# Cross-attention's orders of work on five engines replaced by others, the mask's load set between the context's halves

## What is computed

```python
qp = (q @ Wq.T + bq).reshape(b, t_q, h, d // h).transpose(0, 2, 1, 3)
kp = (k @ Wk.T + bk).reshape(b, t_kv, h, d // h).transpose(0, 2, 1, 3)
vp = (v @ Wv.T + bv).reshape(b, t_kv, h, d // h).transpose(0, 2, 1, 3)
scores = jnp.einsum('bhqd,bhkd->bhqk', qp, kp) / jnp.sqrt(jnp.float32(d))
mask = (attention_mask == 1)[:, None, :, :]
scores = jnp.where(mask, -jnp.inf, scores)
attn = jax.nn.softmax(scores, axis=-1)
out = jnp.einsum('bhqk,bhkd->bhqd', attn, vp)
```

## Time and profile before

| | us |
|---|---|
| median of 3 runs | 2143.24 |
| lowest and highest | 2141.12 to 2149.68 |
| the profiled execution | 2138.41 |
| its span, first to last instruction | 2136.6 |
| PE busy | 1792.0 |
| DVE busy | 1543.1 |
| POOL busy | 1420.9 |
| ACT busy | 1225.2 |

### The profile page before, as it was taken

One profiled execution on the slowest core, in us unless ns is written; L12 is line 12 of the kernel. 1 busy time (PEld: TensorE's weight loads), 2 busy tenths in 40 slices (PEclk: granted clock), 3 DMA queues, 4 the chain that ended last, 5 costly groups with the idle time before them and its releaser, 6 DMA issues. The chain is left out here.

```text
span 2136.6 us, 63160 instructions
## 1 busy us (share of the span) xinstructions
PE 1792.0 (84%) x24267; PEld 1280.2 (60%) x24267; DVE 1543.1 (72%) x3031; ACT 1225.2 (57%) x1911; POOL 1420.9 (67%) x650
## 2 busy tenths in 40 slices
PE   2689988888888888988889989887868785699996
PEld 1266666666666665666566666565435564588885
DVE  3488888777888788788878888778577767444442
ACT  1377777776667676777667777664534431233331
POOL 3288988888878887888868988775345430244442
PEclk9899999999999998999989999998955655799998
DMA  3467555665566555665566656632633324477784
GB/s 112 112 116 144 117 109 110 140 121 112 106 121 142 112 109 111 137 120 111 108 124 135 116 110 125 131 61 56 206 135 113 116 89 149 138 218 235 215 234 122
DMA packets 173920, 277.69 MB, mean 130 GB/s; under 512 B 60020, under 2 KB 133556, under 8 KB 173379
## 3 DMA queue, kind: packets, MB, share of 16 engines
q1 hardware_dynamic: 164836, 261.74, 52.4%
q0 software_dynamic: 8832, 12.06, 3.0%
HBM read 163.02 MB, written 31.98 MB: 91 GB/s over the span
## 5 line engine op out<-in xcount | busy, mean ns | idle before, releaser
L391 POOL TENSOR_TENSOR p_sum<-p_sum,pT 128x1024 f32<-128x1024 f32 x288 | 702.0, 2438 | 61.1 <-ACT pT L609 44.8
L609 ACT ACTIVATE pT<-scored,lift 128x512 f32<-128x512 f32 (+1 forms) x832 | 545.6, 685 | 250.9 <-PE scored L723 236.5
L487 DVE CUSTOM_DVE_ANT_0 junk<-key_ring,mbias 128x898 bf16<-128x898 f32 (+1 forms) x512 | 510.5, 1023 | 95.8 <-issue 94.5
L723 PE MATMUL scored<-qst,kst 128*128 128x64 f16 x6656 | 318.4, 198 | 141.0 <-DVE qst L500 83.0
L723 PEld LDWEIGHTS scored<-qst,kst 128*128 128x128 f16 x6656 | 266.8, 102 | 242.9 <-issue 185.9
L372 POOL TENSOR_TENSOR cp<-cx,cp 128x768 f16<-128x768 f32 (+1 forms) x128 | 321.2, 2520 | 52.0 <-ACT cp L556 52.0
L507 DVE COPY kst<-mbias 64x6144 f16<-64x6144 f16 (+1 forms) x128 | 347.3, 2733 | 3.0
L689 PE MATMUL key_ring<-wvp,cp 128*128 128x256 f16 (+1 forms) x2496 | 305.0, 273 | 4.8 <-DVE mx L487 3.8
L689 PEld LDWEIGHTS key_ring<-wvp,cp 128*128 128x128 f16 (+1 forms) x2496 | 232.7, 99 | 54.5 <-issue 18.5
L746 PE MATMUL o_acc<-pT,v 128*32 128x128 f32 x6656 | 240.1, 278 | 2.1 <-issue 1.1
L460 DVE SCALAR_TENSOR_TENSOR kl<-key_ring,bks,kh 128x384 f16<-128x384 f32 (+1 forms) x256 | 158.7, 633 | 97.0 <-ACT kh L585 93.9
(11 more groups left out here) (225 smaller groups left out, 2481.0 us busy)
## 6 DMA issues: line engine op xcount, KB each, us to landing
w1p<-wsp SPq DMA_DIRECT2D x23, 1408.0 KB, 8.2
cx<-in_ctxT SPq DMA_DIRECT2D x32, 833.0 KB, 12.8
msk<-in_mask SPq DMA_DIRECT2D x64, 400.2 KB, 8.1
cx<-in_ctxT SPq DMA_DIRECT2D x32, 768.0 KB, 8.9
wsp<-w_parts SPq DMA_DIRECT2D x24, 704.0 KB, 3.8
w2p<-wsp SPq DMA_DIRECT2D x23, 640.0 KB
kst<-kh SPq DMA_DIRECT2D x256, 52.1 KB, 2.3
kst<-kl SPq DMA_DIRECT2D x256, 52.1 KB, 2.3
```

Source lines behind the costliest of these rows:

```text
L391: pool.tensor_tensor(p_sum[:], p_sum[:], pT[:, u], ALU.add).then_inc(added, 1)
L487: dve.tensor_tensor_reduce(junk[:, n % 2, :, 0:MPAIR[half]], ring[:, at:at + 2, 0:MPAIR[half]], mbias[:, j, MS[2 * half]:MS[2 * half] + 2 ...
L609: act.activation(pT[0:n, u, HALF * half:HALF * half + HALF], scored[0:n, half, :], ACT.Exp, bias=lift[0:n, 0:1], scale=SSCALE).then_inc(ex ...
L723: mm = pe.matmul(scored[0:n, half, S * (h % PAIRS):S * (h % PAIRS) + S], kst[:, place, rows], qst[:, j, h, :], start=True, stop=True, skip ...
```

## The change

The five tables and the table of banks are replaced. The same steps are run; operations, sizes and waits inside a step are as before. In the tables' own words, for SP and POOL, whose lists are short:

```diff
-POOL_ORDER = steps("QB A1 A2 A3 A4 A5 CL0 A6 A7 A8 A9 CL1 A10 CL2 CL3")
+POOL_ORDER = steps("QB A1 A2 A3 A4 A5 A6 CL0 A7 A8 A9 CL1 A10 CL2 CL3")
-SP_ORDER = steps("CX0 CX1 QS MK QR ST0 ST1")
+SP_ORDER = steps("CX0 MK CX1 QR ST0 QS ST1")
```

More of the change, by code:

```diff
@@ L88, in steps @@
     return [(w.rstrip("0123456789"), int("0" + w.lstrip("ABCDEFGHIJKLMNOPQRSTUVWXYZ"))) for w in text.split()]
[L91 to L95, removed]
-POOL_ORDER = steps("QB A1 A2 A3 A4 A5 CL0 A6 A7 A8 A9 CL1 A10 CL2 CL3")
-DVE_ORDER = steps("MA3 N KL0 KL1 R X0 KL2 X1 KL3 KL4 X2 X3 KL5 X4 X5 KL6 X6 X7 KL7 X8 X9 X10 X11 X12 X13 MA2 X14 X15 SH MA0 MA1 SPR")
-SP_ORDER = steps("CX0 CX1 QS MK QR ST0 ST1")
-BANK = {("K", 0): 3, ("K", 1): 2, ("K", 2): 4, ("K", 3): 3, ("K", 4): 2, ("K", 5): 4, ("K", 6): 4, ("K", 7): 4,
+PE_ORDER = steps("S0 S1 K0 K1 S2 K2 S3 O M0 S4 S5 K3 S6 M1 K4 W0 S7 S8 K5 M2 M3 S9 S10 W1 W2 W3 S11 M4 M5 S12 K6 S13 S14 M6 M7 W4 S15 K7  "
+                 "M8 M9 S16 W5 W6 S17 V0 S18 S19 W7 M10 M11 S20 V1 S21 M12 M13 S22 W8 W9 S23 V2 S24 W10 W11 S25 M14 M15 V3 V4 V5 T V6  "
+                 "W12")
+ACT_ORDER = steps("E0 E1 KH0 KH1 E2 E3 E4 E5 KH2 E6 KH3 KH4 E7 E8 KH5 E9 E10 E11 E12 KH6 E13 CH0 E14 E15 KH7 E16 E17 VH0 E18 CH1 E19 E20  "
+                  "E21 VH1 E22 E23 CH2 VH2 MB VH3 VH4 CH3 E24 E25 VH5 VH6")
+POOL_ORDER = steps("QB A1 A2 A3 A4 A5 A6 CL0 A7 A8 A9 CL1 A10 CL2 CL3")
+DVE_ORDER = steps("MA3 N KL0 KL1 X0 R X1 KL2 KL3 KL4 X2 X3 KL5 X4 X5 KL6 X6 X7 X8 KL7 X9 MA2 X10 X11 X12 X13 MA1 X14 X15 SH MA0 SPR")
+SP_ORDER = steps("CX0 MK CX1 QR ST0 QS ST1")
+BANK = {("K", 0): 1, ("K", 1): 3, ("K", 2): 4, ("K", 3): 3, ("K", 4): 2, ("K", 5): 4, ("K", 6): 4, ("K", 7): 4,
         ("M", 0): 0, ("M", 1): 0, ("M", 2): 0, ("M", 3): 2, ("M", 4): 0, ("M", 5): 2, ("M", 6): 0, ("M", 7): 2,
         ("M", 8): 0, ("M", 9): 2, ("M", 10): 2, ("M", 11): 0, ("M", 12): 2, ("M", 13): 0, ("M", 14): 0, ("M", 15): 2,
[1 row of a table removed]
[1 row of a table added]
 def holders():
```

## The result

| | before | after |
|---|---|---|
| median on the same chip | 2142.18 us | 2184.82 us |
| lowest and highest, 4 runs each | 2139.57 to 2149.68 | 2166.97 to 2185.22 |
| ratio, 95% interval | | 1.0191 [1.014, 1.0242] |
| the profiled execution, its span | 2138.41, 2136.6 | 2184.76, 2183.0 |

The account below looks back on a forecast made before the run. No engine is full; a circle through POOL, PE and ACT sets the pace. 36.98 + 0.9 + 0.14 + 6.64 = 44.66 us a period against 43.44, over 30 periods, gives 2180 us; range 2122 to 2215.

Parts of the forecast that it names:

- the fourth meeting: On POOL, MA3 takes its turn ahead of CL3, so four mask copies meet POOL's steps each period, about 1.6 us each.
- Term 1: At S0, SPR comes one copy earlier, so CL3's end to K0 falls from 1.65 to 0.14 us; gain 1.5 us a period.
- Term 2: On POOL, A1 to CL3's end, work rises from 34.56 to 36.98 us with MA3 ahead of CL3; cost 2.4 us a period.
- rival 1: On POOL, MA3 stays off CL3; three meetings, 35.18 us of work, period 42.9 us, 2127 us in all; chance 0.22.
- Term 3: On PE, K2 ahead of S3 delays E3 and A1; K0 to A1 6.64 us against 5.38, cost 1.3 us a period.
- Term 4: On POOL, waits for `pT` fall from 1.75 to 0.9 us a period; gain 0.85 us.
- rival 3: DVE or PE becomes the bound, X11 holding M13 and M14 so the adds wait; 46.0 us a period, 2220 us; chance 0.07.
- Term 5: On SP, QS and MK move past CX1, QR and ST0; costed at nothing, neither gain nor loss.
- Term 6: On POOL, CL0 moves behind A6; the same sum of work, costed at nothing.

Follow-up runs that it names:

- b_dve: The kernel before with only DVE's copies moved as in the change (MA2 between X9 and X10, MA1 ahead of X14): 2193.98 us, ratio 1.023.
- a_dve: The changed kernel with only DVE's copies put back (MA2 behind X13, MA0 and MA1 between SH and SPR): 2146.51 us, ratio 1.0044.
- a_sp: The changed kernel with SP's old order (CX0 CX1 QS MK QR ST0 ST1): 2200.06 us, ratio 1.0243.
- a_unroll: The changed kernel with four periods in the loop instead of two, six jumps back instead of 13: 2172.21 us, ratio 1.0168.
- a_free: The changed kernel with KH steps waiting only for the transfers that read kh, no longer for the copy kst<-kst: 2163.84 us, ratio 1.0108.
- a_free_unroll: The changed kernel with KH waiting only for transfers that read kh and four periods in the loop: 2143.42 us, ratio 1.0017.
- b_free_unroll: The kernel before with KH waiting only for transfers that read kh and four periods in the loop: 2125.49 us, ratio 0.9914.

## Why the prediction was right, and where it was wrong

**The time and the sign held**: 2184.8 us against 2180, 1.0191. That is in good part luck, as the terms show: against after, the sum has 2.7 us too much work and 1.3 us too much from K0 to A1, 2.3 us too little of waits and 2.0 us too little from CL3's end to K0, and these cancel to 0.3 us. What held of the mechanism is that SPR comes ahead of CL3's end, and the fourth meeting with its price where it occurs, in 3 periods of 29.

*Term 1, S0 earlier, gain 1.5 us: missed.* The distance from CL3's end to K0 went from 1.65 to 2.16 us. The DVE side is as forecast: SPR ends ahead of CL3. The step that failed is "this falls to what K0 needs when CL3 is last". It took for granted that PE is done with its list by then, as in the earlier trace rows, where PE idles 3.60 and 2.96 us. That idle time was cover for the loop's jump, which none of the rows shown names, though three S0 of before's trace do (457.30 above). In the periods of after with the jump the distance is 4.14 us, in the others 0.62.

*Term 2, the fourth meeting, cost 2.4 us: missed as a mean.* The work is 34.24 us, below before's 34.81. (The prediction's 34.56 takes the waits of 25 periods, 1.75 us, from a mean over 29; over the same 29 the waits are 1.50. Its cost would be 2.2 us, and the sum, which starts from 36.98, stays.) The pattern exists, in the first three periods of after. POOL, DVE and PE there:

```profile
164.00 2.35 POOL L388 TENSOR_TENSOR p_sum<-pT 128x1024 f32<-128x1024 f32 x1 [6.11 <-ACT pT L609]
...
194.53 6.81 POOL L372 TENSOR_TENSOR cp<-cx,cp 128x768 f16<-128x768 f32 x2
201.30 0.67 POOL L378 TENSOR_TENSOR qh<-qh_all,sel_q 128x256 f16<-128x256 f16 x1
```

```profile
192.66 3.54 DVE L507 COPY kst<-mbias 64x6144 f16<-64x6144 f16 x1
196.23 1.21 DVE L500 TENSOR_SCALAR qst<-key_ring 1x1024 f16<-1x1024 f32 x1
197.47 2.13 DVE L507 COPY kst<-mbias 64x7184 f16<-64x7184 f16 x1
```

```profile
197.90 0.64 PE L723 MATMUL scored<-qst,kst 128*128 128x64 f16 x16 [0.78 <-DVE qst L500]
201.40 2.10 PE L678 MATMUL key_ring<-cp,wkp 128*128 128x384 f16 x6 [2.85 <-POOL cp L372]
```

This is the prediction word for word: MA3 at 197.47 ahead of CL3, S0 3.4 us early, K0 at 201.40, 0.06 us behind CL3's end, work 37.16, 37.30 and 36.93 us, K0 to A1 6.67, 6.82 and 4.38 us. It lasts until SH comes later. From then on MA0 meets CL3 itself, CL3 follows it at once, and SPR ends only 0.31 to 0.49 us ahead of CL3's end, so MA3 falls on QB. The failed step is "MA0 is issued while CL1 or A10 runs, as now": the delay of SH was named, and put at 1 us. The record's rival 1 has this very case ("SH ends after CL2 has begun").

*Rival 1* therefore describes how copies and POOL meet in 26 periods of 29, and its work, 35.18 us, was even too high. Its time, 2127 us, is far off, because it kept the prediction's 0.9 and 0.14 us for the two terms that grew.

*Term 3, K2 ahead of S3, cost 1.3 us: missed.* K0 to A1 is 5.37 us, as before. The exchange costs 0.4 us, and the lower clock, on which 6.64 us rest, is there behind the jump (6.24 us) and in the first two periods; in the others it is 4.37 us.

*Term 4, waits for `pT`, gain 0.85 us: wrong sign.* They went from 1.42 to 1.88 us a period, and POOL's waits as a whole from 1.50 to 3.17. The rest is CL3's wait for CH3, 1.27 us a period, for which the sum has no term: it moves CH0 and costs the other CH steps at nothing, without a reason. ACT's waits for `cx` did go, as forecast (16.1 us before, none after). The warning stood in the record: it would be wrong "if POOL shows waits of over 2 us a period among the adds" (from 332 to 1450 us the adds wait 55.1 us in 25 periods, 2.2 us each). It stood in rival 3 too, X11 holding M13, with a chance of 0.07; the runs b_dve and a_dve show the moved copies to be the start of the loss. What rival 3 lacked is the jump, KH4 and CH3.

*Term 5, SP's order, nothing*: it holds as far as a_sp can tell. QS lands 2.2 to 5.7 us after its issue, and over 4 us ahead of S0 in every period. *Term 6, CL0 behind A6, nothing*: CL0 waits in no period of after. It was not tried alone.

**The rule of the skill.** Copy and POOL step do take turns: a CL step takes 1.64 us alone and 3.17 us behind a copy, an add 2.36 and up to 3.98 us. The Trainium skill (SBUF — State Buffer, "Who interferes with whom") says that, and the rows of both kernels agree. But the weight that the prediction gave it, that a fourth meeting decides, did not carry: where the meetings fell (fewer CL steps slowed) the kernel still lost.

The cause, as far as it is shown: moving MA1 and MA2 on DVE makes the loss (shown both ways, b_dve and a_dve). They delay M12 and M13, PE ends its list when CL3 does and the jump is exposed (its place is shown by a_unroll), and short periods run into ST1's copy (shown by a_free). These two together are about half of the loss, a_free_unroll against b_free_unroll. The other half is open; the traces show CL3 waiting for CH3 there, which no run tried.

## What to carry to other kernels

An idle time that is named as a wait for one engine may cover something else that waits beside it, a jump or a transfer: before you cost a wait's end at zero, ask what the idle engine has yet to do there, and look for one execution of the place in which that wait comes first. When a loop holds two or more copies of the same period, average them apart, since a cost that comes once per jump shows as a difference between them. And a step moved off the path to one engine's end moves onto the path of whoever it now stands ahead of: here X10 and X11, and so M12 and M13, were the ones to price. And an edit that takes a cost out of the changed kernel says how much of the loss it is only when the same edit is made in the kernel before.

## What the hardware showed besides

The jump back of a loop whose body is long cost PE 2.8 to 3.5 us of standing idle with no semaphore to wait for, 13 times in after, and none in the periods without a jump between them. Halving the jumps removed just those (a_unroll), and gave the kernel before 0.6% [0.2, 1.0] although only three of its jumps delayed S0, by 0.6 to 0.7 us. The Trainium skill (Runtime: NRT & Kernel Launch, "Instruction fetch mechanics") says that a taken branch to a place that is not in the window of fetched pages stops the engine until a transfer has brought it; it gives no duration, and the rows agree with the rule.

PE also stands inside its list for "issue", at about the same place in both kernels, around S15 and W4: 36 us in 22 of 29 periods before, 44 us in 27 after (the 21.1 us ahead of W steps are in part what stood ahead of S steps before). Every such stretch of over 0.3 us, 33 before and 32 after, wherever in the list, has a packet of the instruction queue that begins 2.2 to 3.5 us ahead of its end. So this too goes with a fetch of instructions. How much of it is on the path no run separates.

The 16 transfers of a stack and their copy keep SP issuing for 11.6 us, and the copy lands 6.8 us after its issue in the median. A semaphore that counts this copy too held ACT for 40.5 us in 13 periods; one that counts only the transfers that read ACT's buffer did not hold it at all (a_free).
